# A graph network on one core: x normalised among the edge groups, one root moved up, two weight tiles copied whole

## What is computed

```
h = relu(layernorm(x));  x += mean of h and three rounds of smoothing     # norm = dinv[src]*dinv[dst]
h = relu(layernorm(x));  x += h @ W_self.T + b + (weighted neighbour sum / degree) @ W_neigh.T
h = relu(layernorm(x));  x += gated Chebyshev convolution, two propagations over -dis[src]*w*dis[dst]
h = relu(layernorm(x));  x += graph attention, 4 heads, softmax over the edges of one node
```

## Time and profile before

| | |
|---|---|
| median of three runs | 2469.12 us |
| profiled execution, its own time | 2467.79 us |
| span of its instructions | 2466.0 us |
| busy: PE, VectorE (DVE), ScalarE (ACT), GpSimd (POOL) | 1337.8, 1780.5, 646.5, 1563.2 us |
| group phase | up to about 1549 us |
| propagations | about 1376 to 2050 us |
| attention | about 2050 to 2466 us |

### The profile page before, as it was taken

One profiled execution on the slowest core, in us unless ns is written; L12 is line 12 of the kernel. 1 busy time (PEld: TensorE's weight loads), 2 busy tenths in 40 slices (PEclk: granted clock), 3 DMA queues, 4 the chain that ended last, 5 costly groups with the idle time before them and its releaser, 6 DMA issues. The chain is left out here.

```text
span 2466.0 us, 41573 instructions
## 1 busy us (share of the span) xinstructions
PE 1337.8 (54%) x13050; PEld 748.3 (30%) x13050; DVE 1780.5 (72%) x3952; ACT 646.5 (26%) x1920; POOL 1563.2 (63%) x1191
## 2 busy tenths in 40 slices
PE   2333322333223332233320561699989998999998
PEld 2222222222222222222220120233434443333334
DVE  8999999999999999999993100102321257999996
ACT  0000000013323223221220112100000136888884
POOL 1688888888888888888888777000000037888884
PEclk6555555555555555555555785899999998999997
DMA  5566666456566666665446797999999775333331
GB/s 197 160 181 192 160 177 197 107 144 177 160 193 180 161 189 177 168 183 137 107 108 203 234 357 211 365 370 357 367 397 344 282 246 161 107 105 106 105 107 52
DMA packets 255849, 489.05 MB, mean 198 GB/s; under 512 B 130773, under 2 KB 138620, under 8 KB 246044
## 3 DMA queue, kind: packets, MB, share of 16 engines
q1 hardware_dynamic: 115292, 236.69, 27.7%
q10 hardware_dynamic: 26000, 245.78, 25.0%
q0 software_dynamic: 114480, 5.67, 12.1%
HBM read 320.15 MB, written 167.91 MB: 198 GB/s over the span
## 5 line engine op out<-in xcount | busy, mean ns | idle before, releaser
L1168 POOL DMA_INDIRECT table<-held x782 | 1216.1, 1555 | 322.9 <-issue 310.1
L668 DVE SCALAR_TENSOR_TENSOR resident<-banks,ring,resident 128x1280 bf16<-128x1280 f32 (+9 forms) x790 | 694.3, 946 | 0.3 <-DVE ring L654 0.3
L998 PE MATMUL banks<-ident,held 128*128 128x128 f32 x790 | 189.1, 426 | 869.1 <-DVE held L680 868.0
L998 PEld LDWEIGHTS banks<-ident,held 128*128 128x128 f32 x790 | 157.6, 225 | 876.4 <-DVE held L680 874.9
L1117 PE MATMUL banks<-ring,scaled 128*64 128x512 f32 x1250 | 315.7, 617 | 151.4 <-DMA ring<-counts_dram 71.7
L1378 DVE TENSOR_TENSOR att<-att,banks_d 128x1024 f32<-128x1024 f32 (+1 forms) x350 | 366.1, 1085 | 32.1 <-POOL att L1443 24.8
L1443 POOL TENSOR_SCALAR att<-att 128x1024 f32<-128x1024 f32 (+1 forms) x350 | 320.4, 934 | 81.5 <-ACT att L1346 81.4
L441 ACT ACTIVATE held<-held 128x128 f32<-128x128 f32 x575 | 171.9, 301 | 759.3 <-DMA weights_dram<-held 750.6
L1346 ACT ACTIVATE att<-banks_d 128x1024 f32<-128x1024 f32 (+1 forms) x350 | 302.3, 915 | 75.5 <-PE banks_d L1466 75.5
L1216 POOL DMA_DIRECT2D parts_dram<-scaled x7 | 5.5, 779 | 446.4 <-DVE scaled L853 446.3
L660 DVE SCALAR_TENSOR_TENSOR scaled<-banks,ring,resident 128x1280 bf16<-128x1280 f32 x156 | 235.7, 1548 | 18.2 <-PE banks L998 14.7
(11 more groups left out here) (223 smaller groups left out, 1457.2 us busy)
## 6 DMA issues: line engine op xcount, KB each, us to landing
table<-acc ACTq DMA_DIRECT2D x100, 800.0 KB
held<-table ACTq DMA_DIRECT2D x24, 3200.0 KB
ring<-counts_dram SPq DMA_DIRECT2D x60, 1280.0 KB, 13.5
ring<-weights_dram SPq DMA_DIRECT2D x60, 1280.0 KB, 11.8
weights_dram<-held ACTq DMA_DIRECT2D x25, 1600.0 KB, 9.1
counts_dram<-c_tile ACTq DMA_DIRECT2D x24, 1600.0 KB, 5.5
count<-counts_dram SPq DMA_DIRECT2D x150, 256.0 KB, 2.7
table<-held POOLq DMA_INDIRECT x782, 3.0
```

Of the source, the lines that this page charges most:

```text
L668: ins = nc.vector.scalar_tensor_tensor(equal[b][:, OWN_AT[j]:OWN_AT[j + 1]], key_row[b][:, j * P:GE], keys[:, bass.ds(g * G + j, 1)], own_ ...
L998: ins = nc.tensor.transpose(key_row[b][:, j * P:(j + 1) * P], keys_now[:, b, j:j + 1].to_broadcast([P, P]), k["ident"][:])
L1168: nc.gpsimd.indirect_dma_start(out=table, out_offset=bass.IndirectOffsetOnAxis(ap=cell[:, slot, j:j + 1], axis=0), in_=amount[:, slot, j, ...
```

## The change

VectorE chooses group 1's cells ahead of `compare_own(2)`. After the first round (group 14's compares) it normalises x up to the variances, combines the weights and makes `halves_sum`; after the third round (group 38's) it finishes the normalisation. What was centred in its own buffer is now centred in `h`, and the squares go to the buffer of the counts' copy. ScalarE takes the root of the variances between the last tile's zeroing and the first tile's load, and the two turned matrices and the root of the degrees one tile sooner, before it loads tile 20. The weights of tiles 23 and 24 are copied whole, without sums; VectorE sums them by two `tensor_reduce` of 3200 elements, tile 23's after block 4's sums and tile 24's ahead of the old sum. The halves of tile 24 become 10 and 15 rows instead of 12 and 13. The two copy buffers are viewed as five runs of 640 words, which lie side by side as before.

```diff
@@ ScalarE
                 zero_tile(t)
+            act.wait_ge(var_ready_a, 1)
+            nc.scalar.activation(stat[:, 2], stat[:, 1], ACT.Sqrt).then_inc(std_ready_a, 1)
...
-            with act.Fori(0, T // 4 - 1) as q:
+            with act.Fori(0, T // 4 - 2) as q:
                 for j in range(4):
                     pass_on(q, j)
+            for j in range(3):
+                pass_on(T // 4 - 2, j)
             act.wait_ge(turned_ready, 1)
             nc.scalar.copy(k["w_neigh"][:], turned[:, 0, 0:D]).then_inc(turned_copied, 1)
             nc.scalar.copy(k["w_self"][0:D, :], turned[0:D, 0, D:2 * D]).then_inc(turned_copied, 1)
             act.wait_ge(deg_ready, 1)
             nc.scalar.activation(scale[:, DINV], clipped[:, 0], ACT.Sqrt).then_inc(root_ready, 1)
-            act.wait_ge(var_ready_a, 1)
-            nc.scalar.activation(stat[:, 2], stat[:, 1], ACT.Sqrt).then_inc(std_ready_a, 1)
-
+            pass_on(T // 4 - 2, 3)
             for j in range(2):
                 pass_on(T // 4 - 1, j)
...
-            for s in range(T):
-                ins = nc.scalar.activation(w_tile[:, s], cells[:, s, :, 0], ACT.Copy,
-                                           accum_out=deg_parts[:, s, KEPT_OUT:KEPT_OUT + 1])
-            ins.then_inc(w_split, 1)
+            nc.scalar.copy(w_runs, cells[:, :, :, 0].rearrange("p (q s) c -> p q (s c)", q=PIECES)).then_inc(w_split, 1)
...
             act.wait_ge(w_stored, 16 * T)
+            act.wait_ge(deg_summed, 1)
             for f, half in enumerate(halves):
                 act.wait_ge(half_landed[f], 16)
-                for s in range(half.start, half.stop):
-                    ins = nc.scalar.activation(w_tile[:, s], cells[:, s, :, 0], ACT.Copy,
-                                               accum_out=deg_parts[:, s, T - 1:T])
-                ins.then_inc(w_split, 1)
+                qs = slice(half.start // PIECE, half.stop // PIECE)
+                nc.scalar.copy(w_runs[:, qs], cells[:, half, :, 0].rearrange("p (q s) c -> p q (s c)", s=PIECE)
+                               ).then_inc(w_split, 1)
@@ VectorE
+            def rounds(first, end):
+                with dve.Fori(first, end) as o:
+                    with dve.Fori(1, SLOTS // 2) as i:
+                        next_pair(SLOTS // 2 * o + i, (2 * i - 1, 2 * i))
+                    next_pair(SLOTS // 2 * (o + 1), (SLOTS - 1, 0))
+
             dve.wait_ge(row_ready, 3)
             compare_tail(2, 0)
+            choose_cells(1, 1, 0)
             compare_own(2, 0)
-            choose_cells(1, 1, 0)
-            with dve.Fori(0, ROUNDS) as o:
...
+            rounds(0, 1)
+
+            whole = [P, T, D]
             dve.wait_ge(small_landed, 16 * SMALL)
-            layer_norm(nc, dve, link, x, h, centred_all, stat, var_ready_a, std_ready_a, 0)
-
+            link(nc.vector.tensor_reduce(stat[:, 0], x[:], AX.X, ALU.add))
+            link(nc.vector.scalar_tensor_tensor(h[:], stat[:, 0].unsqueeze(2).to_broadcast(whole), -1.0 / D, x[:],
+                                                ALU.mult, ALU.add))
+            link(nc.vector.tensor_tensor(squares, h[:], h[:], ALU.mult))
+            link(nc.vector.tensor_reduce(stat[:, 1], squares, AX.X, ALU.add))
+            nc.vector.tensor_scalar(stat[:, 1], stat[:, 1], 1.0 / D, EPS, ALU.mult, ALU.add).then_inc(var_ready_a, 1)
             (four operations on cheb0, cheb2 and w_self)
+            nc.vector.tensor_tensor(halves_sum[:], k["ident"][:, 0:D], k["ident"][:, D:2 * D], ALU.add
+                                    ).then_inc(consts_set, 1)
+            rounds(1, 3)
+
+            dve.wait_ge(std_ready_a, 1)
+            link(nc.vector.reciprocal(stat[:, 0], stat[:, 2]))
+            link(nc.vector.scalar_tensor_tensor(h[:], h[:], 0.0, stat[:, 0].unsqueeze(2).to_broadcast(whole),
+                                                ALU.max, ALU.mult))
+            rounds(3, ROUNDS)
...
-            def sum_weights():
-
-                dve.wait_ge(w_split, T + 1)
+            def sum_weights(t, splits):
+
+                dve.wait_ge(w_split, splits)
+                ins = nc.vector.tensor_reduce(deg_parts[:, :, t].rearrange("p (q s) -> p q s", s=PIECE), w_rows, AX.X,
+                                              ALU.add)
+                if t == KEPT_OUT:
+                    ins.then_inc(deg_summed, 1)
+                    return
+                link(ins)
                 nc.vector.tensor_reduce(k["deg_out"][:], deg_parts[:], AX.X, ALU.add).then_inc(deg_summed, 1)
...
                         if NC - 3 <= n < NC - 1:
                             keep_counts(n + 1)
+                        if n == NC - 3:
+                            sum_weights(KEPT_OUT, KEPT_OUT + 1)
                         if n == NC - 1:
-                            sum_weights()
+                            sum_weights(T - 1, T + 1)
```

More of the change, by code:

```diff
@@ L196, in tables_and_products @@
     cells = k["held"][:, 0:2 * NR].rearrange("p (s c two) -> p s c two", c=P, two=2)
-    w_tile = k["held"][:, 2 * NR:3 * NR].rearrange("p (s c) -> p s c", c=P)
+    w_whole = k["held"][:, 2 * NR:3 * NR].rearrange("p (q f) -> p q f", q=PIECES)
+    w_runs = w_whole[:, :, 0:PIECE * P]
+    w_rows = w_runs.rearrange("p q (s c) -> p q s c", c=P)
     zeros = acc[:].rearrange("p t f -> p (t f)")
@@ L230, in tables_and_products @@
     kept = kept_area[:].rearrange("p (q j s c) -> p q j s c", q=4, s=PIECE, c=P)
-    spare = c_tile[:, 1].rearrange("p s c -> p (s c)")[:, 0:math.prod(piece)]
+    second = c_both[:, 1].rearrange("p q f -> p (q f)")
+    spare = second[:, 0:math.prod(piece)]
     resident = [[held[:, q] for q in range(PIECES)],
                 [kept[:, q] for q in range(4)] + [spare.rearrange("p (j s c) -> p j s c", s=PIECE, c=P)]]
-    h_t = c_tile[0:D + 1, 1].rearrange("p s c -> p (s c)")[:, math.prod(piece):math.prod(piece) + BANK]
-    last = c_tile[:, 0]
+    h_t = second[0:D + 1, math.prod(piece):math.prod(piece) + BANK]
+    last = c_rows[:, 0]
     row_parts = xs[:, 0].rearrange("p t f -> p (t f)")[:, 0:3 * BANK].bitcast(BF16).rearrange(
@@ L399, in _ @@
                         sp.wait_ge(sums_ready, NC * (prop - 1) + n + 1)
-                        sp.dma_start(last.rearrange("p s c -> p (s c)"), by_tile(dram)[T - 1]).then_inc(last_landed, 16)
+                        sp.dma_start(c_both[:, 0, :, 0:PIECE * P],
+                                     by_tile(dram)[T - 1].rearrange("p (q f) -> p q f", q=PIECES)).then_inc(last_landed, 16)
         @block.scalar
@@ L440, in split @@
                 for s in range(T):
-                    ins = nc.scalar.activation(w_tile[:, s], cells[:, s, :, 0], ACT.Copy,
+                    ins = nc.scalar.activation(w_rows[:, s // PIECE, s % PIECE], cells[:, s, :, 0], ACT.Copy,
                                                accum_out=deg_parts[:, s, bass.ds(t, 1)])
                 ins.then_inc(w_split, 1)
-                nc.scalar.copy(c_tile[:, b], cells[:, :, :, 1]).then_inc(c_split, 1)
+                nc.scalar.copy(c_both[:, b, :, 0:PIECE * P], cells[:, :, :, 1].rearrange("p (q s) c -> p q (s c)", q=PIECES)
+                               ).then_inc(c_split, 1)
             def store(t, b, at_need=True):
@@ L449, in store @@
                     act.wait_ge(groups_landed, start)
-                for matrix, tile, done in ((counts_dram, c_tile[:, b], c_stored[b]), (weights_dram, w_tile, w_stored)):
-                    act.dma_start(by_tile(matrix)[bass.ds(t, 1)].rearrange("a p f -> (a p) f"),
-                                  tile.rearrange("p s c -> p (s c)")).then_inc(done, 16)
+                for matrix, tile, done in ((counts_dram, c_both[:, b, :, 0:PIECE * P], c_stored[b]),
+                                           (weights_dram, w_runs, w_stored)):
+                    act.dma_start(by_tile(matrix)[bass.ds(t, 1)].rearrange("a p (q f) -> (a p) q f", q=PIECES), tile
+                                  ).then_inc(done, 16)
             def split_done(t):
@@ L824, in keep_counts @@
                     dve.wait_ge(half_landed[f], 16)
-                    nc.vector.tensor_copy(last[:, half], cells[:, half, :, 1]).then_inc(counts_kept, 1)
+                    qs = slice(half.start // PIECE, half.stop // PIECE)
+                    nc.vector.tensor_copy(c_both[:, 0, qs, 0:PIECE * P],
+                                          cells[:, half, :, 1].rearrange("p (q s) c -> p q (s c)", s=PIECE)
+                                          ).then_inc(counts_kept, 1)
             def normalise(ts, tiles, number):
@@ L1107, in _ @@
                         else:
-                            if s in (0, PAIRS) and prop == 0:
-                                pe.wait_ge(counts_kept, 2 + s // PAIRS)
+                            if prop == 0 and s in (halves[0].start, halves[1].start):
+                                pe.wait_ge(counts_kept, 2 if s == 0 else 3)
                             if s == 0 and prop == SAGE:
```

(2 more changed lines are left out.)

49 lines of the change are left out of this document (16 added, 33 removed).

## The result

The changed kernel took 2475.45 us (median of ten runs, 2473.0 to 2478.67); the kernel before, run beside it, 2469.91 (ten runs, 2469.0 to 2472.73). The ratio is 1.0021, 95% interval 1.0012 to 1.0031: the change costs some 5 us. The median of before from which the forecast was made, 2469.12, came from three runs; the ten give 0.8 more. The profiled execution of after took 2475.42 us, its span 2473.6, so it is a middling one. That of before, 2467.79, is lower than each of its ten runs, so the two spans differ by 7.6 where the medians differ by 5.5.

A forecast was written before the change was run, and what follows sets the result against it. The prediction took GpSimd's scatters to bound the kernel, the end moving with their finish. Its terms, -1.0 + 1.3 + 0 - 0.3, summed to 0.0: 2467.8 us by the profile, 2469.1 by the median, range 2461 to 2475.

The forecast's parts named there:

- What bounds the kernel: Whole kernel: the end moves with GpSimd's finish (1549.25) and almost nothing else; PE's work before 1514 is hidden.
- the 8.3 at the end: GpSimd's wait in the last group, over the usual 0.30 each: 8.3 us, forecast to stay.
- Step 1: Start of the group phase: group 1's cells chosen sooner, -1.0 us, bounds -5.0 and +0.5.
- the walk: Scatter-by-scatter reckoning of groups 1 to 4 against the zeroing bursts: group 4 at 138.0 instead of 138.50, -0.5 us.
- Step 2: Group phase: x normalised there, lengthening GpSimd scatters beside VectorE operations, +1.3 us, bounds -1.4 to +4.1.
- The cover: VectorE's lead over GpSimd at group 14: 36 us, of which 25 remain after the added work.
- Step 3: Late group phase: root one tile earlier, SP's stream of counts starting 50 us sooner, 0, bounds -7.6 and +15.8.
- The slower rival: From 1324: SP's stream crowds ScalarE's loads and stores, four starts at 5.85 each, +9.9 us, 2479.0; chance 11%.
- Step 4: Last two tiles: weights copied whole by ScalarE, -0.3 us, bounds -4.4 and +0.5.
- The sum: All terms together: 0.0, so 2467.8 us by the profile and 2469.1 by the median, no change.
- upper edge: Whole kernel: top of the forecast range, 2475 us.
- The faster rival: Group phase: scatters are not held up by zeroing bursts or stream, -5.0 and -3.8 us, 2461.3; chance 13%.

The follow-up runs named there:

- e12: Kernel before, SP's stream of the first five column blocks let out three pieces a group, tile 22's stores issued ahead of tile 23's load: 2463.17 us, ratio 0.9971.
- e7: Kernel before, with SP's stream of the first five column blocks let out three pieces a group: 2470.05 us, ratio 0.9997.
- e11: Kernel before, with tile 22's stores issued ahead of tile 23's load on ScalarE: 2462.74 us, ratio 0.9969.
- e4: Changed kernel, with SP holding block 1's counts in propagation 0 until 70 groups have landed: 2470.57 us, ratio 0.9999.
- e9: Changed kernel, with tile 22's stores issued ahead of tile 23's load on ScalarE: 2467.02 us, ratio 0.9985.
- e1: Kernel before, with only group 1's cells chosen ahead of compare_own(2): 2471.05 us, ratio 1.0002.
- e3: Changed kernel without the earlier choice of cells and the whole copies, so only normalisation and roots are moved: 2473.53 us, ratio 1.0012.
- e6: Changed kernel, with SP's stream of the first five column blocks let out three pieces a group: 2468.51 us, ratio 0.9990.
- e2: Kernel before, with only the weights of tiles 23 and 24 copied whole and summed on VectorE: 2470.99 us, ratio 1.0001.
- e5: Changed kernel, with group 1's cells chosen after compare_own(2) again: 2473.86 us, ratio 1.0008.
- e8: Changed kernel, with SP's stream of column blocks 1 to 3 bringing one of four tiles of each piece: 2464.26 us, ratio 0.9973.

## Why the prediction was wrong

**What bounds the kernel.** Right, and in more kernels than it was made for: over the table the start of the attention layer is 499.1 to 501.7 us behind the last tile's load. PE's early start bought nothing; it waited 42.96 us up to 1544.28, as forecast. But the prediction read GpSimd's finish as the cause of all that follows and took the 8.3 at the end as given "since tile 23's load and tile 22's stores are there as before". That was right for this change. It is also where 7 to 10 us lay open (last load, e12 beside e7 and e11 beside before): the stores needn't have been behind that load.

**Step 1.** Right in its walk. Forecast 78.2, 96.4, 122.2 and 138.0, measured 78.73, 96.71, 121.92 and 138.56, and the first scatter of all came 0.49 later in after (52.45 for 51.96), before any part of the change. Without that each of the four is within 0.8 of the walk. Counted from the first scatter, group 4 starts after 86.06 to 86.13 us in the seven kernels with step 1, and after 86.24 to 86.54 in the seven without: a gain of 0.1 to 0.5, for the walk's 0.5 and the -1.0 in the sum. It is too small for the times to show.

**Step 2.** The cover held: VectorE's groups end at 1323.04 (1324.3 forecast), and between 150 and 1320 no scatter waits over 0.3. The scatters beside VectorE's operations grew as was said. After, the operations of VectorE and the scatters beside them:

```profile
275.63 1.83 DVE L762 SCALAR_TENSOR_TENSOR h<-stat,x_nodes 128x1600 f32<-128x1600 f32 x1
...
276.04 2.84 POOL L1200 DMA_INDIRECT table<-held  x1 [0.30 <-issue]
```
```profile
672.36 1.82 DVE L778 SCALAR_TENSOR_TENSOR h<-h,stat 128x1600 f32<-128x1600 f32 x1
...
673.04 2.57 POOL L1200 DMA_INDIRECT table<-held  x1 [0.30 <-issue]
```

With one of 1.79 at 1326.16, beside the scaling of the rows, that is 2.6 over three of 1.55. Gone are 1.44 at 1371.91 and 0.5 at another that the prediction had overlooked (2.06 at 1313.97). Net +0.6 where +1.3 was taken. Two of the three operations that moved were hit, not all three.

**Step 3, the step that failed:** "The stream has the same bytes and meets GpSimd 50 us earlier: about as many starts. 0". The waits at starts went from 17.1 to 20.4, +3.3, inside the bounds of -7.6 and +15.8 but not nothing. The bytes were the same and so was the count: of nine starts from 1320 to 1500 six waited, in both kernels. What changed was the price of one: 2.9 on the mean before, 3.4 after. The prediction had priced four starts after 1400 at 13.5 and left those around the pause out of both sides: before, 1329.21 waits 2.04, 1347.78 and 1366.34 nothing, and 1387.64 with 1392.04 2.54. In the pause ScalarE's load of tile 20 and stores of tile 19 had the DMA engines for themselves, at 144 GB/s, and were through before the next start. In after they lie on the stream (load issued at 1334.89, stores at 1356.34), and the starts behind them wait 4.66 and 4.17. Two starts met the stream together with ScalarE's traffic before (1412.74, 1434.73), four do after (1355.05, 1377.48, 1421.33, 1443.46); in exchange the starts that waited at 1455.15 and 1476.11 go free. That is where 11.1 us of lag fell back to 4.5. e4 shows that it is the pause: with it put back, the starts fall to 16.7, and the time is that of before.

The slower rival, at 11%, had this mechanism and was right in it: four crowded starts. It took them at 5.85 each, where they wait 3.5 to 4.9 over the usual, and wanted to decide only from a mean of 4.6 up. It took less to leave no change behind: 3.3 here and 0.6 in step 2, with next to nothing gained in step 1 to pay for them.

**Step 4.** Right: nothing, alone and in sum. The weights of tile 24 are stored 23.6 us behind its load in e9 and 28.1 in e11, and the attention layer begins 500.0 and 501.3 behind that load. 4.5 us earlier on ScalarE are at most 1.3 at the end. Over all kernels the layer begins 499.1 to 501.7 us behind the load in the eight with step 4, and 500.3 to 501.3 in the six without.

**The sum.** Forecast -1.0, +1.3, 0, -0.3. Measured up to the last load: 0.1 (the late first scatter and step 1 together), 0.6, 3.3, together 4.0 of the 4.49. The 0.5 left is spread evenly over the 630 scatters between groups 4 and 68, less than 0.001 us each; e1 and e3 have it too, while e4 and e6, which are after there line for line, have none: it differs from execution to execution. The last load fell at 1553.74, inside the 1554.1 up to which the forecast said it would stand; the end did not. The profiled spans differ by another 2.9, all in the attention layer:

```profile
2054.30:2104.70 50.40, 49.45 (x293) 0.90 0.64 175
```

That is the layer's first 50 us in after (length, PE busy and count, granted clock, DMA share, GB/s). Before it was 0.94 there, in e4 0.94, in e7 0.93, in e3 0.90, in e1, e2, e5, e6 and e8 to e12 0.88 or 0.89, in kernels that share every line of this layer. How much of the time PE is granted its full clock differs from one execution to another; the profiled run of before had a good one. Of the 5.5 between the medians some 4.7 are there when the layer begins, and the rest is within what ten runs tell. The forecast had no term for it. Its upper edge lay 5.9 above the predicted time, the measured time 6.3: 0.8 of that is the median of before, which three runs had put low. So the failed step alone would have stayed inside the range; what took the time past the edge, by 0.45, was the rest beside it.

**The faster rival** took the scatters for not held up, and put the rule of turns beside it. The Trainium skill (DMA: Bandwidth & Descriptors, Queues, rings and completion order) has it that an engine changes between its queues after each packet. The waits here don't contradict that an engine takes turns, but turns don't spare a scatter: beside bulk traffic of 230 GB/s or more a start waits 1.2 to 8.3 us over the usual, and 14.7 MB more in another queue cost 11.2.

## What to carry to other kernels

Where indirect scatters pace a phase and wait for each other's landing, bulk traffic that is still moving when a wait falls due has a price: here 1.2 us and more a time, and 0.8 us a MB on the mean of e8. To start such traffic sooner is no gift, unless somebody waits for it. A pause of one stream may be what lets another through: before closing it, list each start that falls in it, with its wait of zero. And look for a stretch in which the DMA engines are empty just ahead of one in which they are full: here a store stood behind a load that waited for something else, and two lines swapped gave back more than the whole change had cost.

## What the runs showed of the hardware

What holds a scatter's landing up is the traffic of the last few us before a start, not how much passed since the start before. In e6 a batch of 3.9 MB let out at 1355 together with ScalarE's stores was still moving at 1370 (318 GB/s in the 6 us before the start was due), and the start at 1374.41 waited 2.84; the batch at 1376.7 alone was down by 1390, and the next start waited 0.30. The granted clock of the first 50 us of the attention layer was 0.88 to 0.94 in fourteen profiles of kernels that are the same there; from its first fetch to the end of the span the layer took 416.4 us at 0.94 (before), 419.3 at 0.90 (after) and 420.1 at 0.89 (e11). The three at 0.93 or 0.94 took 416.4 to 418.2, the eleven at 0.88 to 0.90 418.8 to 421.6.
